# Attention steps in four places of a group, a reordered head, and the last down weights in w_ops

## The chip, the cores and the metric

The kernel runs on one core of a Trainium2 chip. Its time is the device time of one execution in microseconds; a profiled execution also gives a span, from the first to the last instruction, and a record of each engine: TensorE (PE), VectorE (DVE), ScalarE (ACT), GpSimd (POOL) and SyncE (SP), which here issues all DMAs.

## What is computed

```python
x = L0_attn_x                        # 1 x 2048 x 512, float32
xn = _layernorm(x, axis=-1)
# attention "over the heads of one token": 32 query heads, 8 key and value heads, D = 16
q = einsum('bse,edh->bsdh', xn, Wq) + bq
k = einsum('bse,edh->bsdh', xn, Wk) + bk   # k and v repeated 4 times along h
v = einsum('bse,edh->bsdh', xn, Wv) + bv
scores = einsum('bsdh,bseh->bsde', q, k) / sqrt(D)
s = einsum('bsde,bseh->bsdh', softmax(scores), v).reshape(...)
# gated feed-forward, inner size 1792
nx = xn * rsqrt(mean(xn * xn) + 1e-5) * ln_w
y = (silu(nx @ gate_w.T) * (nx @ up_w.T)) @ down_w.T
out = x + s * silu(y)
```

Scores are 16 x 16 for each token, so attention is no work for TensorE: VectorE does it by products and reductions.

## The kernel before

Each float32 operand is split into a high part (rounded to a format of TensorE, written by ACT) and a low part (the rest, written by VectorE or GpSimd); a product is then three matmuls, high x high, high x low, low x high. The 2048 rows go in 2 pairs of 1024; a pair is two blocks of 512 (4 tiles of 128 each). The inner size is 14 chunks of 128, so there are `GROUPS` = 28 groups: a group is one chunk of one pair, for both blocks.

**A group.** Gate and up for both blocks are a 2 x 2 block product, done in seven products in the manner of Strassen (m1 to m7, 6 matmuls of 512 columns each) instead of eight; groups 0 and 14 are plain (gate0, up0, gate1, up1, 12 matmuls each). TensorE's order in a group is m1, m5, m6, m2, m7, one down product (12 matmuls), m4, m3: 54 matmuls. Between them ACT copies the running sum into another bank (`seed`, L782, for which m6 waits), `take_u2` (L797, for m7), `silu0`, `take_u3`, and `silu1` of the group before (L806). VectorE does `c12` of the group before behind its m3 (L1068), `times_up1` of the group before (L1079), `c22` (L1064) and `times_up0` (L1073, which needs m4). ACT's `h_hi_part` and GpSimd's `h_lo_part` (L413) then split the product h.

**Weights.** In the first pair each chunk's weights are loaded raw, scaled, combined (`sums`, L1028) and split (`hi_a`, `lo_a`, `hi_s`, `lo_s`; `hi_wd` and GpSimd's `wd_lo_part` for the down weights), and written to DRAM; later use loads them back. `w_ops` has two slots of chunk weights, `wd_ops` three slots of down weights, filled in turn by `load_wd` (L309). There are `ITEMS` = 56 down products; those beyond 41 come behind the last group.

**Attention.** A tile's attention is 13 steps of VectorE, in one fixed sequence over all tiles (`attn_place`): six for scores (product, reduction, product, reduction, row maximum, subtraction) and seven for values (product, reduction, product, reduction, row sum, reciprocal, scaling). Between them ACT takes an exponential for a pair of tiles (`exps`, L827), for which the first value step waits; exponential and silu need different tables on ACT. There are 208 steps. `attention(n)` (L1131) runs the next n. `PAIR_SHARES` (L240) says how many run at each of three places of each group, `BURST_SHARES` at nine places between the pairs; what is left runs behind the last group.

**Head.** Before group 1 the first eight tiles of x are normalised and transposed, QKV is computed for them (`qkv_product`, taken from the bank by VectorE's `qkv_take`), and four combined operands are made: `t_add` (DVE), `t_hi` (ACT), `t_lo` (DVE). The order on every engine is written out by hand; waits are counts of semaphores. Each engine runs its instructions in that order, so a waiting one holds up all behind it.

**End.** `y_out` (ACT, L833) takes the silu of an output tile; `finish` (DVE, L1139) multiplies it by the attention result and adds x; SyncE stores it.

## Time and profile before

| | us |
|---|---|
| median of 3 runs | 500.21 (499.72 to 500.76) |
| profiled execution | 499.32 |
| its span | 497.5 |
| TensorE busy | 474.6 (95%) |
| VectorE busy | 409.6 (82%) |
| ScalarE busy | 229.3 (46%) |
| GpSimd busy | 121.7 (24%) |

The mean granted clock of TensorE is 0.991 of full speed. Busy time counts each engine by itself; the engines overlap. Matmuls are pipelined: one is shown longer than the distance to the next, and the distance is its cost. Where an engine stood idle before a row, the row may end with the idle time and with what ended it.

### The profile page before, as it was taken

Reading aid. Unit: us, or ns where it says so; the run is one execution under the profiler, and the core shown is the slowest. Engines: PE = TensorE matmul, PEld = TensorE weight load, DVE = VectorE, ACT = ScalarE, POOL = GpSimd, SP = SyncE. Lnnn points to the kernel's source line nnn. Section 1 sums busy time; section 2 is a strip of 40 time slices with the busy share of each in tenths; the row PEclk is TensorE's granted clock in tenths of the full one; section 3 lists DMA queues with packets and bytes.
Section 4 is the critical chain, followed back from the end, with each engine's and each line's share of the span. In section 5 each row is a group of like instructions: output and inputs, shape, how many; then the busy total and the mean of one; then the engine's idle time right before and its main releaser. Section 6 shows DMA issues by size and latency. Waiting matters only on the chain.

```text
span 497.5 us, 6152 instructions
## 1 busy us (share of the span) xinstructions
PE 474.6 (95%) x2148; PEld 392.4 (79%) x2148; DVE 409.6 (82%) x538; ACT 229.3 (46%) x379; POOL 121.7 (24%) x104
## 2 busy tenths in 40 slices
PE   7797999999999999999999999999999999999980
PEld 6696888778778888888898888888888888888870
DVE  7679688888898798749999767986888697699996
ACT  4683565576577554394114263224322532547010
POOL 3713121121222182242232111111111111139600
PEclk9999999999999999999999999999999999999996
DMA  8802799666666755683354559555556545415552
GB/s 280 301 1 88 283 319 393 239 250 251 238 248 241 273 221 209 230 343 114 121 186 164 190 193 359 192 199 219 207 198 214 224 182 198 163 50 203 182 200 85
DMA packets 27311, 105.12 MB, mean 211 GB/s; under 512 B 2833, under 2 KB 4113, under 8 KB 23953
## 3 DMA queue, kind: packets, MB, share of 16 engines
q1 hardware_dynamic: 27280, 104.74, 57.6%
q8 instruction: 17, 0.28, 0.2%
q14 instruction: 14, 0.11, 0.1%
HBM read 68.29 MB, written 36.44 MB: 210 GB/s over the span
## 4 chain that ended last, share of the span: by engine, by line
PE 68%; DVE 15%; issue 8%; ACT 3%; SPq 2%; POOL 2%; DMA 1%; DVEq 0%; ACTq 0%; POOLq 0%
PE gu_ps L469 14%; PE gu_ps L472 13%; PE gu_ps L471 13%; PE y_ps L596 6%; PE y_ps L598 6%; PE y_ps L597 6%; DVE prod L1119 2%; PE gu_ps L618 2%; PE gu_ps L619 2%; PE gu_ps L622 2%; DVE attn L1122 2%; DVE prod L1101 2%; DVE xz L1146 1%; DMA bias<-bv 1%; SPq L266 1%
## 5 line engine op out<-in xcount | busy, mean ns | idle before, releaser
L469 PE MATMUL gu_ps<-z_hi,w_ops 128*128 128x512 f32 x364 | 143.3, 394 | 0.4
L472 PE MATMUL gu_ps<-z_hi,w_ops 128*128 128x512 f32 x364 | 141.8, 389 | 0.0
L471 PE MATMUL gu_ps<-z_lo,w_ops 128*128 128x512 f32 x364 | 141.7, 389 | 0.0
L420 POOL TENSOR_TENSOR h_lo<-h,h_hi 128x512 fp32r<-128x512 f32 x28 | 37.8, 1351 | 200.6 <-ACT h_hi L825 200.6
L469 PEld LDWEIGHTS gu_ps<-z_hi,w_ops 128*128 128x128 f32 x364 | 68.3, 188 | 19.7 <-ACT u L800 5.0
L472 PEld LDWEIGHTS gu_ps<-z_hi,w_ops 128*128 128x128 f32 x364 | 68.3, 188 | 14.3
L471 PEld LDWEIGHTS gu_ps<-z_lo,w_ops 128*128 128x128 f32 x364 | 68.3, 188 | 13.6
L596 PE MATMUL y_ps<-wd_ops,h_hi 128*128 128x512 f32 x168 | 65.9, 392 | 0.1
L598 PE MATMUL y_ps<-wd_ops,h_lo 128*128 128x512 f32 x168 | 65.6, 391 | 0.0
L597 PE MATMUL y_ps<-wd_ops,h_hi 128*128 128x512 f32 x168 | 65.5, 390 | 0.0
L825 ACT ACTIVATE h_hi<-h 128x512 fp32r<-128x512 f32 x28 | 17.7, 631 | 81.9 <-DVE h L1077 81.9
L1119 DVE TENSOR_TENSOR prod<-scores,qkv 128x1024 f32<-128x1024 f32 x32 | 43.5, 1358 | 0.8
L1101 DVE TENSOR_TENSOR prod<-qkv 128x1024 f32<-128x1024 f32 x32 | 42.9, 1341 | 0.5
L424 POOL TENSOR_TENSOR wd_ops<-raw,wd_ops 128x512 fp32r<-128x512 f32 x14 | 20.1, 1436 | 88.5 <-ACT wd_ops L748 88.5
L1122 DVE TENSOR_REDUCE attn<-prod 128x64 f32<-128x1024 f32 x32 | 38.9, 1216 | 0.8
L1104 DVE TENSOR_REDUCE scores<-prod 128x128 f32<-128x1024 f32 x32 | 38.9, 1216 | 0.8
L598 PEld LDWEIGHTS y_ps<-wd_ops,h_lo 128*128 128x128 f32 x168 | 31.5, 188 | 6.7
L596 PEld LDWEIGHTS y_ps<-wd_ops,h_hi 128*128 128x128 f32 x168 | 31.5, 188 | 6.6 <-POOL h_lo L420 0.3
L597 PEld LDWEIGHTS y_ps<-wd_ops,h_hi 128*128 128x128 f32 x168 | 31.6, 188 | 6.3
L1089 DVE TENSOR_TENSOR h_kept<-u 128x512 f32<-128x512 f32 x26 | 19.0, 730 | 19.4 <-ACT u L813 19.3
L420 POOL TENSOR_TENSOR h_lo<-h_kept,h_hi 128x512 fp32r<-128x512 f32 x15 | 20.3, 1354 | 45.1 <-ACT h_hi L825 45.1
L800 ACT ACTIVATE u<-gu_ps 128x512 f32<-128x512 f32 x26 | 15.6, 600 | 29.3 <-PE gu_ps L472 19.3
(120 smaller groups left out, 769.2 us busy)
## 6 DMA issues: line engine op xcount, KB each, us to landing
w_kept<-w_ops SPq DMA_DIRECT2D x13, 1792.0 KB, 5.7
w_ops<-w_kept SPq DMA_DIRECT2D x13, 1792.0 KB, 7.5
wd_ops<-wd_kept SPq DMA_DIRECT2D x42, 512.0 KB, 3.5
raw<-gate_up SPq DMA_DIRECT2D x28, 256.0 KB, 3.6
wd_kept<-wd_ops SPq DMA_DIRECT2D x14, 512.0 KB, 7.2
xz<-x SPq DMA_DIRECT2D x16, 256.0 KB, 5.9
raw<-down SPq DMA_DIRECT2D x14, 256.0 KB, 7.4
xz<-x SPq DMA_DIRECT2D x2, 1024.0 KB, 5.7
```

The lines of the kernel that those rows point to most:

```text
L420: pool.tensor_tensor(lo, src, hi.bitcast(F32), ALU.subtract).then_inc(h_lo_done, 1)
L424: pool.tensor_tensor(wd_ops[:, n % 3, 1, :], wd_raw[:, n % 2, :], wd_ops[:, n % 3, 0, :].bitcast(F32), ALU.subtract).then_inc(wd_lo_done, 1)
L469: pe.matmul(acc, w_h, z_hi[:, zi, c, :], start=start and c == 0, stop=False, skip_group_check=True)
L471: pe.matmul(acc, w_h, z_lo[:, zi, c, :], start=False, stop=False, skip_group_check=True)
L472: end = pe.matmul(acc, w_l, z_hi[:, zi, c, :], start=False, stop=c == 1, skip_group_check=True)
L596: pe.matmul(acc, hi, wd_ops[:, u % 3, 0, :], start=n == 0, stop=False)
L597: pe.matmul(acc, hi, wd_ops[:, u % 3, 1, :], start=False, stop=False)
L598: pe.matmul(acc, lo, wd_ops[:, u % 3, 0, :], start=False, stop=n == NI - 1).then_inc(d_done, 1)
L1101: return dve.tensor_tensor(pr, q[:, d:d + HALF, :].unsqueeze(2).to_broadcast([P, HALF, D, HKV]), k.unsqueeze(1).to_broadcast([P, HALF, D, ...
L1104: return dve.tensor_reduce(s[:, d:d + HALF, :], pr, X, ALU.add)
L1119: return dve.tensor_tensor(pr, e[:, d:d + HALF, :].unsqueeze(2).to_broadcast([P, HALF, HKV, D]), v.unsqueeze(1).to_broadcast([P, HALF, HKV ...
L1122: return dve.tensor_reduce(o[:, d:d + HALF, :], pr, X, ALU.add)
```

## The change

1. **Four places.** Each group has a fourth place for attention steps, behind `times_up0`. The table is new; it sums to 49 and 130 steps for the two pairs instead of 42 and 104, so with the burst's 29 all 208 are placed. For example group 15 has (0, 7, 3, 1) instead of (0, 3, 2), group 16 (0, 5, 3, 0) instead of (1, 5, 2), group 26 (0, 6, 4, 0) and group 27 (2, 6, 3, 1) instead of (1, 5, 2). In the first pair GpSimd's `wd_lo_part` also waits for the first reduction of its group's second place.
2. **Order in a group.** ACT does `silu1` ahead of `seed`; in the first pair `hi_wd` and mostly `hi_s` move forward, and VectorE does `times_up1` ahead of `sums`.
3. **Head.** The query weights come in two loads and are summed and split in halves; the biases are loaded ahead of x tiles 5 to 7; up0(0) starts on the high weights; QKV products 0 and 7, down product 0, and many operations of ACT and VectorE change places.
4. **Late down weights.** Down products 49 to 55 have seven places of their own in `w_ops`, loaded once m3 of the last group is done.

```diff
+        LATE = ITEMS - 7
+        w_late = w_ops[:].rearrange("p a s m n -> p (a s m n)").rearrange("p (u s n) -> p u s n", u=7, s=2)
+
+        def wd_place(u):
+            return w_late[:, u - LATE] if u >= LATE else wd_ops[:, u % 3]
...
+        PAIR_SHARES = (((0, 0, 0, 0), (0, 0, 0, 0), (0, 0, 1, 0), (1, 3, 2, 0), (1, 2, 1, 1), (0, 3, 1, 0),
...
+                       ((0, 3, 4, 0), (0, 7, 3, 1), (0, 5, 3, 0), (0, 6, 2, 0), (1, 6, 2, 1), (0, 5, 3, 0),
...
+        def first_reduce(g):
+            before = attn_before(g) + shares[g][0]
+            return next((q for q in range(before, before + shares[g][1]) if places[q][2] in (1, 3)), 0)
...
+            def load_late_wd(u):
+                sp.wait_ge(m3_done, GROUPS)
+                sp.dma_start(wd_place(u).rearrange("p s n -> p (s n)").bitcast(F32), wd_kept[item(u)[1]])\
+                  .then_inc(wd_late_loaded[u - LATE], 16)
...
-            sp.dma_start(wq_raw, wq.rearrange("(k p) n -> p k n", p=P)).then_inc(wq_in, 16)
+            for a in (0, 2):
+                sp.dma_start(wq_raw[:, a:a + 2, :], wq.rearrange("(k p) n -> p k n", p=P)[:, a:a + 2, :])\
+                  .then_inc(wq_in[a // 2], 16)
...
-            load_x(0, range(J, JJ))
+            load_x(0, (J,))
...
+            load_x(0, range(J + 1, JJ))
...
-            for u in range(ITEMS - NI, ITEMS):
+            for u in range(ITEMS - NI, LATE):
                 load_wd(u)
+            for u in range(LATE, ITEMS):
+                load_late_wd(u)
...
             def wd_lo_part(n):
                 pool.wait_ge(wd_hi_done, n + 1)
+                wait(pool, attn_step, first_reduce(n))
...
+            def first_up0():
+                pe.wait_ge(w_hi_a, 2)
+                for n, (wi, zi, c) in enumerate(chunks):
+                    w_h = w_ops[:, 0, 0, wi, c * P:(c + 1) * P]
+                    pe.matmul(acc, w_h, z_hi[:, zi, c, :], start=n == 0, stop=False)
+                    pe.matmul(acc, w_h, z_lo[:, zi, c, :], start=False, stop=False)
+                pe.wait_ge(w_lo_a, 2)
...
             first_gate0()
-            up0(0)
+            first_up0()
+            qkv_product(0)
             second_tile(J)
-            qkv_product(0)
+            qkv_product(1)
             second_tile(J + 1)
-            qkv_product(1)
             second_tile(J + 2)
...
-            for index in range(4, JJ - 1):
+            for index in range(4, JJ):
                 qkv_product(index)
-            down_product(0)
...
+            h_hi_part(0)
+            hi_wd(0)
             z_hi_tile(0, J + 3)
...
+            t_hi(0, 0)
             silu1(0)
-            h_hi_part(0)
-            for n in range(3):
-                t_hi(0, n)
-            hi_wd(0)
+            t_hi(0, 1)
+            t_hi(0, 2)
             hi_s(1)
+            scale(2, (0, 1))
             t_hi(0, 3)
-            scale(2, (0, 1))
             for g in range(1, NI):
-                seed(g)
                 if g >= 2:
                     silu1(g - 1)
+                seed(g)
...
             for g in range(NI + 1, GROUPS):
-                seed(g)
                 if g > NI + 1:
                     silu1(g - 1)
+                seed(g)
...
                 attention(shares[g][2])
                 times_up0(g)
+                attention(shares[g][3])
             c12(LAST)
             times_up1(LAST)
-            attention(6)
-            assert taken[0] >= values_end(3 * J - 1)
+            attention(STEPS)
             for j in range(J):
                 finish(2, j)
-                attention(4)
-            attention(STEPS)
```

How the instructions stand in a row, at three places. First ACT at the start of group 4, before and after; the row with `h_hi<-h` ends group 3's work, `gu_ps<-gu_ps` is the seed, `u<-u` is `silu1` (its wait: `c12_done`), `w_ops<-raw` of 768 is `hi_a`:

```order
L825 ACTIVATE h_hi<-h 128x512 [waits d_done,h0_done]
L788 ACTIVATE gu_ps<-gu_ps 128x512 [waits c12_done,m1_done]
L813 ACTIVATE u<-u 128x512 [waits c12_done]
L735 ACTIVATE w_ops<-raw 128x768 [waits gu_scaled,w_stored1,m3_done]
L800 ACTIVATE u<-gu_ps 128x512 [waits h1_done,m6_done]
L795 ACTIVATE h<-gu_ps 128x512 [waits h_lo_done,m2_done]
L804 ACTIVATE u<-gu_ps 128x512 [waits m7_done]
```

```order
L868 ACTIVATE h_hi<-h 128x512 [waits d_done,h0_done]
L856 ACTIVATE u<-u 128x512 [waits c12_done]
L831 ACTIVATE gu_ps<-gu_ps 128x512 [waits c12_done,m1_done]
L778 ACTIVATE w_ops<-raw 128x768 [waits gu_scaled,w_stored1,m3_done]
L791 ACTIVATE wd_ops<-raw 128x512 [waits wd_stored1,d_done,wd_in0]
L843 ACTIVATE u<-gu_ps 128x512 [waits h1_done,m6_done]
L838 ACTIVATE h<-gu_ps 128x512 [waits h_lo_done,m2_done]
```

`silu1` and the seed have changed places, and `hi_wd` has come forward.

Then VectorE near the end of the head, before (from `t_lo` to the takes of QKV products 5 and 6) and after (from the last of the sums to the last operation ahead of group 1); `z_lo<-h_kept` is `t_lo`, `h_kept<-h_kept` is `t_add`, `qkv<-gu_ps` a take, `h_kept<-u,gu_ps` is `times_up1(0)`:

```order
L1025 TENSOR_TENSOR z_lo<-h_kept,z_hi 128x1024 [waits t_hi_done]
L1020 TENSOR_TENSOR h_kept<-h_kept 128x2x512 [waits t_added]
L1025 TENSOR_TENSOR z_lo<-h_kept,z_hi 128x1024 [waits t_hi_done] x2
L1042 TENSOR_TENSOR w_ops<-raw,w_ops 128x768 [waits w_hi_a]
L1061 SCALAR_TENSOR_TENSOR qkv<-gu_ps,rms,bias 128x384 [waits rms_done,qkv_done]
L1033 TENSOR_TENSOR raw<-raw 128x256 [waits gu_scaled]
L1034 TENSOR_TENSOR raw<-raw 128x256
L1036 TENSOR_TENSOR raw<-raw 128x256 [waits w_summed]
L1038 TENSOR_TENSOR raw<-raw 128x256 [waits w_summed]
L1089 TENSOR_TENSOR h_kept<-u,gu_ps 128x512 [waits m3_done,silu1_done]
L1061 SCALAR_TENSOR_TENSOR qkv<-gu_ps,rms,bias 128x384 [waits rms_done,qkv_done] x2
```

```order
L1089 TENSOR_TENSOR raw<-raw 128x256 [waits w_summed]
L1140 TENSOR_TENSOR h_kept<-u,gu_ps 128x512 [waits m3_done,silu1_done]
L1112 SCALAR_TENSOR_TENSOR qkv<-gu_ps,rms,bias 128x384 [waits rms_done,qkv_done]
L1076 TENSOR_TENSOR z_lo<-h_kept,z_hi 128x1024 [waits t_hi_done]
L1112 SCALAR_TENSOR_TENSOR qkv<-gu_ps,rms,bias 128x384 [waits rms_done,qkv_done]
L1076 TENSOR_TENSOR z_lo<-h_kept,z_hi 128x1024 [waits t_hi_done]
L1100 TENSOR_TENSOR w_ops<-raw,w_ops 128x1024 [waits w_hi_s]
L1112 SCALAR_TENSOR_TENSOR qkv<-gu_ps,rms,bias 128x384 [waits rms_done,qkv_done]
L1076 TENSOR_TENSOR z_lo<-h_kept,z_hi 128x1024 [waits t_hi_done]
L1112 SCALAR_TENSOR_TENSOR qkv<-gu_ps,rms,bias 128x384 [waits rms_done,qkv_done]
L1071 TENSOR_TENSOR h_kept<-h_kept 128x2x512 [waits t_added]
```

The take of product 4 now stands ahead of all `t_lo`, and the fourth `t_add` is the last operation of the head.

Then VectorE in group 15, from `t_lo(1, 3)` (`z_lo<-raw`) to its c12 before, and from the same operation to the last step ahead of `times_up0(15)` after; `u<-gu_ps,u` is c22 (wait `u3_done`) or c12:

```order
L1025 TENSOR_TENSOR z_lo<-raw,z_hi 128x1024 [waits t_hi_done]
L1119 TENSOR_TENSOR prod<-scores,qkv 128x1024 [waits attn_step]
L1122 TENSOR_REDUCE attn<-prod 128x64 [waits attn_step]
L1124 TENSOR_REDUCE row_sum<-scores 128x16 [waits attn_step]
L1066 TENSOR_TENSOR u<-gu_ps,u 128x512 [waits u3_done]
L1126 RECIPROCAL row_inv<-row_sum 128x16 [waits attn_step]
L1127 TENSOR_TENSOR attn<-attn,row_inv 128x128 [waits attn_step]
L1077 TENSOR_TENSOR h<-h,gu_ps 128x512 [waits silu0_done,m4_done]
L1071 TENSOR_TENSOR u<-gu_ps,u 128x512 [waits u2_done,m3_done]
```

```order
L1076 TENSOR_TENSOR z_lo<-raw,z_hi 128x1024 [waits t_hi_done]
L1170 TENSOR_TENSOR prod<-scores,qkv 128x1024 [waits attn_step]
L1173 TENSOR_REDUCE attn<-prod 128x64 [waits attn_step]
L1175 TENSOR_REDUCE row_sum<-scores 128x16 [waits attn_step]
L1177 RECIPROCAL row_inv<-row_sum 128x16 [waits attn_step]
L1178 TENSOR_TENSOR attn<-attn,row_inv 128x128 [waits attn_step]
L1152 TENSOR_TENSOR prod<-qkv 128x1024 [waits qkv_out,attn_step]
L1155 TENSOR_REDUCE scores<-prod 128x128 [waits attn_step]
L1117 TENSOR_TENSOR u<-gu_ps,u 128x512 [waits u3_done]
L1152 TENSOR_TENSOR prod<-qkv 128x1024 [waits attn_step]
L1155 TENSOR_REDUCE scores<-prod 128x128 [waits attn_step]
L1157 TENSOR_REDUCE row_max<-scores 128x16 [waits attn_step]
```

Ten steps stand between `t_lo(1, 3)` and `times_up0(15)`, where five stood.

## Rows read from the trace of the kernel before

**Rows 1.** The page, busy us, share of the span and instructions of each engine.

```profile
PE 474.6 (95%) x2148; PEld 392.4 (79%) x2148; DVE 409.6 (82%) x538; ACT 229.3 (46%) x379; POOL 121.7 (24%) x104
```

**Rows 2.** Who waited for whom (us in total, times, longest).

```profile
PE gu_ps L618 <- issue: 3.5, 1, 3.5
PE gu_ps L488 <- DVE w_ops L1042: 2.5, 1, 2.5
```

**Rows 3.** Timeline of the end: start us, duration us, engine, line, operation, tiles.

```profile
480.42 0.47 PE L596 MATMUL gu_ps<-wd_ops,z_hi 128*128 128x512 f32 x1 [1.26 <-DMA wd_ops<-wd_kept]
...
485.00 1.23 DVE L1119 TENSOR_TENSOR prod<-scores,qkv 128x1024 f32<-128x1024 f32 x1
...
485.75 0.39 PE L598 MATMUL gu_ps<-wd_ops,z_lo 128*128 128x512 f32 x1
486.17 0.60 ACT L841 ACTIVATE xz<-gu_ps 128x512 f32<-128x512 f32 x1 [0.76 <-PE gu_ps L598]
486.26 1.22 DVE L1122 TENSOR_REDUCE attn<-prod 128x64 f32<-128x1024 f32 x1
...
488.47 0.68 DVE L1146 TENSOR_TENSOR xz<-xz,attn 128x512 f32<-128x512 f32 x1
...
493.24 0.69 DVE L1150 TENSOR_TENSOR xz<-xz 128x512 f32<-128x512 f32 x1
```

**Rows 4.** Timeline between the pairs and of group 14.

```profile
269.04 0.63 ACT L831 ACTIVATE scores<-scores 128x512 f32<-128x512 f32 x1
...
277.30 0.68 DVE L1077 TENSOR_TENSOR h<-h,gu_ps 128x512 f32<-128x512 f32 x1
...
280.44 0.39 PE L488 MATMUL gu_ps<-z_hi,w_ops 128*128 128x512 f32 x1
...
283.15 0.39 PE L469 MATMUL gu_ps<-z_hi,w_ops 128*128 128x512 f32 x1
...
286.29 1.23 DVE L1025 TENSOR_TENSOR z_lo<-raw,z_hi 128x1024 fp32r<-128x1024 f32 x1 [2.15 <-ACT z_hi L780]
```

**Rows 5.** The page, DMA issues: count, KB each, median us from issue to landing.

```profile
wd_ops<-wd_kept SPq DMA_DIRECT2D x42, 512.0 KB, 3.5
```

**Rows 6.** Timeline of the head, all engines.

```profile
13.90 0.63 ACT L735 ACTIVATE w_ops<-raw 128x512 fp32r<-128x512 f32 x1
...
15.62 0.67 DVE L1042 TENSOR_TENSOR w_ops<-raw,w_ops 128x512 fp32r<-128x512 f32 x1
...
16.35 0.50 PE L488 MATMUL gu_ps<-z_hi,w_ops 128*128 128x512 f32 x1 [2.46 <-DVE w_ops L1042]
...
30.29 3.62 DVE L1020 TENSOR_TENSOR h_kept<-h_kept 128x1024 f32<-128x1024 f32 x3 [0.67 <-ACT h_kept L770]
...
42.85 0.60 DVE L1061 SCALAR_TENSOR_TENSOR qkv<-gu_ps,rms,bias 128x384 f32<-128x384 f32 x1
...
43.55 0.41 PE L618 MATMUL gu_ps<-wqkv_hi,z_hi 128*128 128x384 f32 x1 [3.53 <-issue]
```

**Rows 7.** Timeline of group 4, where m7 starts late.

```profile
86.83 1.34 POOL L420 TENSOR_TENSOR h_lo<-h,h_hi 128x512 fp32r<-128x512 f32 x1 [4.81 <-ACT h_hi L825]
86.93 1.52 DVE L1034 TENSOR_TENSOR raw<-raw 128x256 f32<-128x256 f32 x1
...
89.94 0.60 ACT L800 ACTIVATE u<-gu_ps 128x512 f32<-128x512 f32 x1 [1.31 <-DVE h_kept L1089]
...
90.60 0.50 PE L469 MATMUL gu_ps<-z_hi,w_ops 128*128 128x512 f32 x1
```

**Rows 8.** Groups 15 to 26: stretch and length, busy us of PE, PEld, DVE, ACT, POOL.

```profile
283.15:431.13 147.98, 147.98 (x649) 121.31 (x648) 115.27 (x145) 56.42 (x87) 14.25 (x11) 1.00 0.59 217
```

**Rows 9.** Timeline of ACT and VectorE at the end of group 26.

```profile
429.98 0.69 DVE L1077 TENSOR_TENSOR h<-h,gu_ps 128x512 f32<-128x512 f32 x1 [1.24 <-PE gu_ps L472]
...
431.33 0.69 DVE L1071 TENSOR_TENSOR u<-gu_ps,u 128x512 f32<-128x512 f32 x1 [0.67 <-PE gu_ps L472]
...
433.29 1.28 ACT L813 ACT_TABLE_LOAD   x1
```

More of the change, by code:

```diff
@@ L443, in _ @@
                 .then_inc(bias_summed, 1)
-            scale_tile(J + 1)
-            pool.wait_ge(var_done, J + 1)
-            rms_of(0, J, 1, 0)
-            scale_tile(J + 2)
-            scale_tile(J + 3)
+            for j in range(J + 1, JJ):
+                scale_tile(j)
             pool.wait_ge(var_done, JJ + 2)
@@ L514, in first_gate0 @@
                 end.then_inc(m2_done, 1)
+            def first_up0():
+                acc = gu_ps[:, UP_BANK, :]
+                chunks = [(wi, zi, c) for wi, zi in ((WA21, ZB11), (WA22, ZB21)) for c in range(2)]
+                pe.wait_ge(w_hi_a, 2)
[4 more added lines that the diff above has]
+                pe.wait_ge(w_lo_a, 2)
+                for n, (wi, zi, c) in enumerate(chunks):
+                    end = pe.matmul(acc, w_ops[:, 0, 1, wi, c * P:(c + 1) * P], z_hi[:, zi, c, :], start=False,
+                                    stop=n == 3)
+                end.then_inc(m4_done, 1)
             def up0(g):
-                if g:
-                    pe.wait_ge(c12_done, sevens(g))
-                else:
-                    pe.wait_ge(w_lo_a, a_pieces(0))
+                pe.wait_ge(c12_done, sevens(g))
                 eight(gu_ps[:, UP_BANK, :], g, ((WA21, ZB11), (WA22, ZB21))).then_inc(m4_done, 1)
@@ L845, in _, with hi_qkv @@
             act.wait_ge(lnw_in, 16)
+            def hi_qkv(half_of_k):
+                k = slice(2 * half_of_k, 2 * half_of_k + 2)
+                act.wait_ge(wqkv_summed, 2 * half_of_k + 2)
+                act.wait_ge(wkv_in, 32)
+                act.activation(wqkv_hi[:, k, :], wqkv_raw[:, k, :], ACT.Copy).then_inc(wqkv_hi_done, 1)
             scale(0, (0,))
@@ L860, in _ @@
             silu0(0)
+            z_tile(J)
             z_tile(J + 1)
@@ L1208, in _ @@
                 attention(shares[g][0])
-                if g + 1 < NI:
-                    sums(g + 1)
                 if g > 1:
@@ L1213, in _ @@
                 if g + 1 < NI:
+                    sums(g + 1)
                     lo_a(g + 1, WA11, WS1, a_pieces(g + 1))
+                if g == 1:
+                    t_lo(0, 3)
                 if g == 8:
@@ L1228, in _ @@
                 c22(g)
-                if g == 1:
-                    qkv_take(JJ - 1)
                 if g + 1 < NI:
```

121 lines of the change are left out of this document (63 added, 58 removed), and 4 rows, old and new, of the table PAIR_SHARES.

## The prediction

> **What bounds the kernel now.** I read the page's engine line first: TensorE is busy 474.6 of 497.5 us [rows 1], so time can only come from its few gaps and from what lies behind its last matmul. The list of who TensorE waited for gives two large gaps, 3.5 us before a QKV product and 2.5 us before up0(0) [rows 2]; a third, 1.26 us for a down weight, stands in the timeline of the end [rows 3]. In that timeline the last matmul starts at 485.75, the last `y_out` on ACT at 486.17, but VectorE is still doing attention steps; its first closing product starts at 488.47 and its last addition at 493.24, ending at 493.93, and the span ends 3.57 us later with the last store [rows 3]. So the end is set by VectorE, not by TensorE. From 60 us on TensorE runs group after group of 54 matmuls. A matmul of 512 columns starts 0.227 us after the one before: 12 of them, up1(14), take 280.44 to 283.15 [rows 4]. A group is then 12.25 us. I write times inside a group from its first m1 matmul.
>
> **The tail, -5.7.** The new table sums to 179 steps and the burst adds 29: 208, all there are. Before, 33 steps were left behind the last group; a product or a reduction starts 1.26 us after the step ahead of it (485.00, 486.26) [rows 3]. With none left, the last two VectorE operations follow the last `y_out`: 486.17 + 0.60, then 0.7 + 0.7 with their hand-overs, 488.25. Before it was 493.93: -5.7. The four closing pairs take 1.35 us each and the four `y_out` come 1.36 us apart, so they keep pace. The store behind them is unchanged.
>
> **Late down weights, -1.4.** Products 49 to 55 get places of their own in `w_ops`. The wait at 480.42 (1.26 us idle, 1.4 against the pace) goes [rows 3], unless the seven loads come late. On SyncE they stand behind load 48, which waits for product 45; load 49 is then wanted three products (8.2 us) later, and each further one 2.7 us later. A load of this size takes 3.5 us to land (median of 42) [rows 5], so the queue has room. If that cover failed, the old 1.3 us would be back.
>
> **The head, -3.0.** The old up0(0) waited for both halves of its weights. Its high half is ready when ACT ends at 14.53, the low half when VectorE ends at 16.29, and TensorE starts at 16.35 [rows 6]. `first_up0` asks for the high half alone: start 14.6, -1.75. A part is lost again: by my estimate the low QKV weights, now in two pieces with statistics between them, are ready only near 19.2, and gate1(0) waits for the last `z_lo` near 29.2, which follows its `z_hi` on ACT behind `h_hi(0)` and `hi_wd(0)`. I get up1(0) done 1.0 earlier. The 3.5 us gap at 43.55 is a wait for `qkv_take(4)`, which VectorE does at 42.85, behind additions, `t_lo` and `lo_a` [rows 6]. In the new order I start `t_add` at 29.85 instead of 30.29 and add up by like rows: the first addition 1.2 and 0.8 of blocking by `h_lo(0)`, a take 0.55, two additions 2.4 (three took 3.62 [rows 6]), `lo_a` 0.9 (0.67 for two thirds of it at 15.62), four sums 1.45 (0.42 each, overlapping), `times_up1` 0.6, take 0.55, so 38.3. TensorE wants it at 38.8: the gap (3.7 with its restart) goes. But ACT has `t_hi(0, 3)` ahead of `seed(1)`, and `t_add(0, 3)` is now the last operation of VectorE's head, ending near 45.7. The chain behind take 4 is three `t_lo` of 1.2, three takes, `lo_s` 1.1 and that addition, 7.4. With 1.06 for `t_hi` and 0.58 for the seed, m6(1) can start at 47.35, and TensorE is there at 45.65: +1.7. In sum -1.0 - 3.7 + 1.7 = -3.0. Bounds: -4.7 if the seed isn't late, -1.3 if VectorE's head slips 1.7 more (one contended operation costs about 1.1: 1.52 at 86.93 where the same takes 0.42 [rows 7]). The split query load and the earlier RMS cost nothing: behind them ACT waits for the value weights anyway.
>
> **Groups 2 to 13, -2.2.** m7 waits for `u2`, `u2` for `times_up1`, and that stood behind four sums: in group 4 ACT ends `u2` at 90.54 and m7 starts at 90.60, 0.25 behind pace, with 0.1 more at the restart [rows 7]. Five groups have that in full and two in part, with small ones 1.9 in all. `silu1` and `times_up1` now come first, 1.5 us earlier. VectorE's work in the fullest groups (3 and 7) is 5.9 for weights and products and 5.9 attention, 11.8 of 12.25, and `h_lo` on GpSimd runs beside a reduction there. So I take these waits as gone. Group 13's late `times_up0` goes with them (-0.3).
>
> **Groups 15 to 27: -1.1 and +3.8.** The same m7 wait (0.22 in five groups) goes. What comes is VectorE's load. In groups 15 to 26 it was busy 115.3 of 148.0 us [rows 8]; steps added there cost 20.8 more, 136.1 of 147.0. Bounded from the rows of an ordinary group, `times_up0` can start at 11.1, c12 at 12.45 (0.20 of the next) [rows 9]. Where they come late:
> - Burst. It now ends with two value steps of pair 2, which wait for an exponential that ACT reaches only at 269.04 to 269.67 [rows 4]; VectorE is there near 264.8 and stands 5 us. Then two steps, four closing pairs and three steps: `times_up0(14)` ends near 281.1, not 277.98. up1(14) wants it at 280.44: +0.7.
> - Group 15. `t_lo(1, 3)` can't start before 3.14 (286.29, group start 283.15) [rows 4]. Then 7 steps (5.97), c22, 3 steps (2.93): `times_up0` at 13.8 instead of 11.1, c12 at 14.8 instead of 12.45. silu1, seed and m6(16) follow 1.9 behind c12: +1.7.
> - Groups with an exponential (17, 20, 23, 26). ACT now loads the table (1.28, row 433.29 [rows 9]) ahead of the seed, so m6 can start 3.84 behind `times_up0`: just in time if that starts at 11.1, late by what it is late. 0.1 each in three, but group 26 has steps of 3.0 between c22 at 9.2 and `times_up0`: near 12.2, +1.1. Together +1.4.
>
> The sum on the profiled execution: -5.7 - 1.4 - 3.0 - 2.2 - 1.1 + 0.7 + 1.7 + 1.4 = -9.6, so a span of 487.9. The execution took 499.32 where the runs' median is 500.21; I set the forecast against the median: 490.6, rounded 490.5.
>
> **Contention.** A VectorE operation with two inputs in SBUF that meets one of GpSimd waits for it: `raw` at 86.93 took 1.52 instead of 0.42, ending just behind GpSimd's at 88.17 [rows 7]. The Trainium skill (SBUF — State Buffer, Who interferes with whom) states an exclusive lock: whoever is second blocks until the first is done, and reductions never meet it. By that rule the trace agrees; an estimate from it is one whole GpSimd operation for each meeting, against 1.1 from the row.
>
> **Rivals.**
> 1. *The places fit, nothing new is late* (seed in the head, groups 15 and 26 on time, burst too). For it: slack of 10.9 us in twelve groups. Against: the exponential and `t_hi` can't come earlier. It gives 490.5 - 1.7 - 3.8, 485.0. Chance 0.12.
> 2. *VectorE bounds part of the second half.* 136.1 and one meeting with `h_lo` in each of twelve groups (1.1 each) are 149.3 for 147.0: +2.3, and with the forced waits between places another 2. 494.5. Chance 0.10.
> 3. *The head gives next to nothing*: VectorE's head slips further and the first groups run late. +1.7 to +3: 493. Chance 0.10.
> 4. *Slower.* VectorE must wait in order: 0.66 us between `times_up0` and c12 and 0.78 (ACT's silu with its hand-overs) between c12 and `times_up1` where a place is empty [rows 9]. If each group pays 11.35 of work, 1.1 of blocking and both waits, it lasts 13.9 instead of 12.25: 12 x 1.65 is 19.7, less the 2.8 counted, near 507. It decides from 13.1 us a group. Against it: empty places are used in just those groups whose work is less, and blocking mostly meets a reduction. Chance 0.04.
> 5. *The late loads don't hide*, or come in another order: +1.4, 491.9. Inside my range; 0.04.
>
> **How the numbers follow.** The forecast keeps 0.60 (488 to 492.5). Rivals 1, 2 and 3 set the ends: 485.5 to 494.8 leaves out the slower case and a part of 1 and 2. A measurement of this kernel can tell 0.2% (1 us) from no change. Faster holds all but rival 4: 0.95; same 0.01; slower 0.04.
>
> **What would show it.** Right: VectorE's last operation within 1.6 us of the last `y_out`; no gap in the last 13 products; up0(0) near 14.6; no wait before QKV product 6 but one before m6(1) behind `t_hi` and `seed`; a VectorE idle of 5 us before a value product near 265; gaps before up1(14), m6(16), m6(27). Wrong: `times_up0` starting beyond 12 in most groups of the second half, or c12 beyond 13, or a span above 493.

## The result, and the profile after

| | before | changed |
|---|---|---|
| median, us | 499.97 (4 runs, 498.80 to 500.76) | 488.71 (4 runs, 488.14 to 488.76) |
| ratio of the times, 95% interval | | 0.977 (0.975 to 0.980) |
| profiled execution, its span | 499.32, 497.5 | 488.14, 486.4 |

The forecast was 490.5. The prediction's sum was made against the profiled execution: a span of 487.9 was foretold, and 486.4 was measured. Busy time on the page of the changed kernel, the line that answers to [rows 1]:

```profile
PE 473.5 (97%) x2148; PEld 394.6 (81%) x2148; DVE 395.4 (81%) x539; ACT 227.1 (47%) x378; POOL 119.4 (25%) x106
```

TensorE has the same work in 11 us less. What it waited for, in all 486 us (us in total, times, longest), against [rows 2]; two waits of 0.3 and 0.2 us are left out:

```profile
PE gu_ps L502 <- ACT gu_ps L831: 3.6, 4, 1.2
PE y_ps L687 <- POOL ident L419: 1.5, 1, 1.5
PE gu_ps L539 <- ACT z_hi L806: 1.2, 1, 1.2
PE gu_ps L521 <- DVE z_lo L1051: 0.9, 1, 0.9
PE gu_ps L521 <- DVE h L1128: 0.5, 1, 0.5
```

The waits of 3.5 and 2.5 us are gone. What is left is mostly one kind: m6 (L502) waits four times for the seed (L831).

Where the 11.1 us of span went is read from the start of the same down product in both timelines. In the changed kernel down product 1 (in group 2), 12 (in group 13), 27 (between the halves of group 14) and the first one behind the last group start at

```profile
63.12 0.39 PE L643 MATMUL y_ps<-wd_ops,h_hi 128*128 128x512 f32 x1
...
198.04 0.39 PE L643 MATMUL y_ps<-wd_ops,h_hi 128*128 128x512 f32 x1
...
268.61 0.39 PE L643 MATMUL y_ps<-wd_ops,h_hi 128*128 128x512 f32 x1
...
440.87 0.39 PE L643 MATMUL gu_ps<-wd_ops,h_hi 128*128 128x512 f32 x1
```

where the kernel before has 67.08, 204.37, 275.00 and 443.62. The lead is 3.96, 6.33, 6.39 and 2.75, and 4.31 at the last matmul (481.44, before 485.75). The entries are rounded one by one, and so don't add up to the last digit:

| stretch | prediction | measured |
|---|---|---|
| head, up to group 2 | -3.0 | -4.0 |
| groups 2 to 13 | -2.2 | -2.4 |
| groups 14 to 27 | +2.7 | +3.6 |
| last down weights | -1.4 | -1.6 |
| VectorE behind the last matmul | -5.7 | -5.7 |
| from VectorE's end to the span's end | 0 | -1.1 |
| sum | -9.6 | -11.1 |

The first row holds the start of the execution too: the first gate product begins at 11.45 in this trace and at 10.92 in the one before, so counted from there the head gave 4.5.

The end of the changed kernel, which answers to [rows 3]:

```profile
481.44 0.39 PE L645 MATMUL gu_ps<-w_ops,z_lo 128*128 128x512 f32 x1
481.87 0.60 ACT L884 ACTIVATE xz<-gu_ps 128x512 f32<-128x512 f32 x1 [0.76 <-PE gu_ps L645]
...
483.23 0.69 DVE L1201 TENSOR_TENSOR xz<-xz 128x512 f32<-128x512 f32 x1
```

VectorE's last operation starts 1.8 us behind the last matmul, before it was 7.5. The last `y_out` now sets it.

### The profile page after: what moved, and what is told of

It is laid out like the page before. It is cut to its first block, busy times and chain, and to the rows that moved or that the text cites. A ratio compares the mean times of both kernels' runs of the same rounds, so it can differ in the third digit from the quotient of the medians.

```text
span 486.4 us, 6166 instructions
## 1 busy us (share of the span) xinstructions
PE 473.5 (97%) x2148; PEld 394.6 (81%) x2148; DVE 395.4 (81%) x539; ACT 227.1 (47%) x378; POOL 119.4 (25%) x106
## 4 chain that ended last, share of the span: by engine, by line
PE 77%; DVE 11%; ACT 5%; issue 4%; DMA 1%; SPq 0%; POOL 0%; ACTq 0%; DVEq 0%
PE gu_ps L502 15%; PE gu_ps L505 15%; PE gu_ps L504 15%; PE y_ps L643 7%; PE y_ps L645 7%; PE y_ps L644 7%; PE gu_ps L644 3%; PE gu_ps L643 3%; PE gu_ps L645 3%; DVE prod L1170 1%; PE gu_ps L665 1%; PE gu_ps L666 1%; PE gu_ps L669 1%; DVE attn L1173 1%; DVE z_lo L1076 1%
## 5 line engine op out<-in xcount | busy, mean ns | idle before, releaser
L502 PE MATMUL gu_ps<-z_hi,w_ops 128*128 128x512 f32 x364 | 142.4, 391 | 3.6 <-ACT gu_ps L831 3.6
L447 POOL TENSOR_TENSOR h_lo<-h,h_hi 128x512 fp32r<-128x512 f32 x28 | 38.9, 1389 | 226.3 <-ACT h_hi L868 226.3
L502 PEld LDWEIGHTS gu_ps<-z_hi,w_ops 128*128 128x128 f32 x364 | 68.3, 188 | 20.8 <-issue 6.5
L1170 DVE TENSOR_TENSOR prod<-scores,qkv 128x1024 f32<-128x1024 f32 x32 | 41.8, 1308 | 5.5 <-ACT scores L874 4.8
L1152 DVE TENSOR_TENSOR prod<-qkv 128x1024 f32<-128x1024 f32 x32 | 40.5, 1265 | 0.6
L453 POOL TENSOR_TENSOR wd_ops<-raw,wd_ops 128x512 fp32r<-128x512 f32 x14 | 18.6, 1328 | 64.8 <-ACT wd_ops L791 28.7
L1197 DVE TENSOR_TENSOR xz<-xz,attn 128x512 f32<-128x512 f32 x16 | 15.4, 962 | 21.5 <-ACT xz L884 21.5
L1140 DVE TENSOR_TENSOR h_kept<-u 128x512 f32<-128x512 f32 x26 | 20.0, 771 | 14.2 <-ACT u L856 10.7
```

Of the source, the lines that this page charges most:

```text
L447: pool.tensor_tensor(lo, src, hi.bitcast(F32), ALU.subtract).then_inc(h_lo_done, 1)
L502: pe.matmul(acc, w_h, z_hi[:, zi, c, :], start=start and c == 0, stop=False, skip_group_check=True)
L1140: dve.tensor_tensor(h_kept[:, g % NI, :], u2[:], up, ALU.mult).then_inc(h1_done, 1)
L1152: return dve.tensor_tensor(pr, q[:, d:d + HALF, :].unsqueeze(2).to_broadcast([P, HALF, D, HKV]), k.unsqueeze(1).to_broadcast([P, HALF, D, ...
L1170: return dve.tensor_tensor(pr, e[:, d:d + HALF, :].unsqueeze(2).to_broadcast([P, HALF, HKV, D]), v.unsqueeze(1).to_broadcast([P, HALF, HKV ...
```

## The experiments

All are timed in five rounds beside the kernel before. "Against changed" is the difference to the changed kernel's 488.7, which was measured in other rounds: the kernel before had a median of 499.97 beside it, and of 499.9 to 501.1 beside the others. The last column says which of the texts written before the run came true, the theory or its rival.

| kernel | edit | us | ratio to before (95%) | against changed | result |
|---|---|---|---|---|---|
| up0_waits | changed, up0(0) late | 488.7 | 0.976 (0.974 to 0.978) | 0.0 | theory |
| seed_first | changed, seed(1) first | 487.7 | 0.974 (0.972 to 0.977) | -1.0 | theory |
| table_ahead | changed, silu table early | 486.4 | 0.971 (0.969 to 0.973) | -2.3 | theory |
| places_old | changed, old table and end | 491.7 | 0.982 (0.980 to 0.984) | +3.0 | theory, size off |
| late_off | changed, old slots | 490.2 | 0.981 (0.979 to 0.982) | +1.5 | theory |
| fit15 | changed, burst eased | 487.1 | 0.975 (0.973 to 0.976) | -1.6 | half |
| order_old2 | changed, seed before silu1 | 489.4 | 0.979 (0.977 to 0.981) | +0.7 | first's sign, half its size |
| zhi_first | changed, z_hi first | 488.3 | 0.977 (0.975 to 0.979) | -0.4 | rival, nearly |
| wdlo_free | changed, wd_lo unbound | 490.7 | 0.982 (0.980 to 0.984) | +2.0 | between |
| before_places | before, new places | 497.6 | 0.995 (0.993 to 0.996) | | theory's total, not its terms |
| before_late | before, late weights | 499.9 | 0.999 (0.997 to 1.000) | | theory |
| all_eased | changed, five edits | 482.4 | 0.964 (0.962 to 0.966) | -6.3 | theory |

The start of a profiled execution (when the first gate product begins) varied over these traces from 10.7 to 12.6 us, before any edit acts. The changed kernel's own interval is 0.975 to 0.980. Those of table_ahead, places_old and all_eased lie clear of it and that of wdlo_free touches it; the others overlap it. So for differences under 2 us the starts and gaps of TensorE in the traces decide, and the times only agree with them.

### The head

```diff
             def first_up0():
+                pe.wait_ge(w_lo_a, 2)
...
+            stats_tile(J)
             lo_a(0, WA22, WA21 + 1, 2)
             for j in range(J, JJ):
-                stats_tile(j)
+                if j > J:
+                    stats_tile(j)
```

> The changed kernel (488.7 us, span 486.4) with one part of the head undone: VectorE does the statistics of x tile 4 ahead of the low up weights again, and up0(0) waits for both halves of its weights. My theory: what up0(0) gains by starting early is not what the head gained. The changed kernel's TensorE waits 1.10 us before gate1(0), for a z_lo that does not hang on up0(0), and 0.46 before the first QKV product's low weights. So up0(0) will start near 16.3 instead of 14.3, gate1(0) at 28.8 to 29.3 instead of 28.83, and m6(1) at 46.7 as now, since its seed stands behind t_hi(0,3), which waits for VectorE's fourth t_add. Time 488.7, +0.5 at most. Rival: the early start is carried through, then the time is 2.0 longer, 490.7.

TensorE's first up product and m6(1) in this run:

```profile
15.45 0.50 PE L556 MATMUL gu_ps<-z_hi,w_ops 128*128 128x512 f32 x1 [1.13 <-DVE w_ops L1094]
...
46.55 0.47 PE L502 MATMUL gu_ps<-z_hi,w_ops 128*128 128x512 f32 x1 [1.04 <-ACT gu_ps L832]
```

up0(0) starts 1.2 later than the changed kernel's 14.29 (not 2.0: x tile 4 was there earlier than before), and m6(1) not later than its 46.70. The early start of up0(0) is worth nothing by itself: the next wait, 1.10 us before gate1(0) in the changed kernel, takes it up (0.21 here).

```diff
+            seed(1)
             t_hi(0, 3)
             for g in range(1, NI):
                 if g >= 2:
                     silu1(g - 1)
-                seed(g)
+                    seed(g)
```

> The changed kernel with seed(1) ahead of t_hi(0,3) on ScalarE, nothing else. My theory: m6(1) waits 1.2 us in the changed kernel only because the seed stands behind t_hi(0,3), which ends at 45.97, while m1(1) is done near 44.1. With the seed first the gap before m6(1) goes, and m4(1), which needs the t_lo of that t_hi, has 6 us more: -1.2, so 487.5 and a span of 485.2. Rival: t_lo(0,3) or the takes behind it are what is late next, in m4(1) or group 2, and less than 0.3 is gained: 488.6.

The changed kernel first: VectorE's fourth `t_add`, ScalarE's `t_hi` and seed, and m6(1).

```profile
43.76 1.22 DVE L1071 TENSOR_TENSOR h_kept<-h_kept 128x1024 f32<-128x1024 f32 x1
...
45.01 1.06 ACT L823 ACTIVATE z_hi<-h_kept 128x1024 fp32r<-128x1024 f32 x1 [5.83 <-DVE h_kept L1071]
45.98 0.58 ACT L831 ACTIVATE gu_ps<-gu_ps 128x512 f32<-128x512 f32 x1
...
46.70 0.47 PE L502 MATMUL gu_ps<-z_hi,w_ops 128*128 128x512 f32 x1 [1.05 <-ACT gu_ps L831]
```

And the seed of the other kernel:

```profile
45.45 0.58 ACT L831 ACTIVATE gu_ps<-gu_ps 128x512 f32<-128x512 f32 x1 [5.12 <-PE gu_ps L505]
```

The seed now waits for TensorE (m1), not TensorE for the seed: of four long m6 waits three are left. In the changed kernel a wait of ScalarE for VectorE, 5.8 us long, had stood ahead of the seed, which needs nothing of it.

```diff
+            z_hi_tile(0, J + 3)
             h_hi_part(0)
             hi_wd(0)
-            z_hi_tile(0, J + 3)
```

> The changed kernel with z_hi of x tile 7 ahead of h_hi(0) and hi_wd(0) on ScalarE in the head. My theory: gate1(0) waits 1.10 us for the last z_lo, because its z_hi stands behind those two operations (26.42 to 27.56). With the z_hi first, that z_lo, the z_raw, the t_add behind it and the whole chain to t_hi(0,3) and m6(1) come 1.0 earlier: -1.0, so 487.7, with m6(1) at 45.7 instead of 46.70. Rival: h_hi(0) and hi_wd(0) then delay GpSimd's two operations into VectorE's t_add, or the chain hangs on other things, and the gap moves to QKV product 6 or stays before m6(1): no change, 488.7.

The gap before gate1(0) went, and the one before m6(1) grew by 0.3. GpSimd's `wd_lo(0)` and `h_lo(0)`, and two of VectorE's `t_add`, in order of time:

```profile
28.49 1.30 POOL L453 TENSOR_TENSOR wd_ops<-raw,wd_ops 128x512 fp32r<-128x512 f32 x1 [4.11 <-ACT wd_ops L791]
...
28.93 1.94 DVE L1071 TENSOR_TENSOR h_kept<-h_kept 128x1024 f32<-128x1024 f32 x1 [0.83 <-ACT h_kept L813]
...
29.74 2.29 POOL L447 TENSOR_TENSOR h_lo<-h,h_hi 128x512 fp32r<-128x512 f32 x1
...
31.32 1.79 DVE L1071 TENSOR_TENSOR h_kept<-h_kept 128x1024 f32<-128x1024 f32 x1
```

An addition takes 1.22 alone. Moved 0.5 earlier, VectorE met GpSimd twice (+0.7 and +0.6), where in the changed kernel it meets it once (+0.6), and lost again most of what it had won. The rival holds but for 0.3: the head hangs on VectorE's chain, not on gate1(0).

The largest part of the head's gain, the 3.7 us ahead of QKV product 6, was not undone by any run. The trace of the kernel before shows two causes. One is the prediction's: the take stands behind other work. The other it left out: in that stretch VectorE met GpSimd twice, a `t_lo` at 38.67 took 2.32 instead of 1.22, and the `lo_a` below 2.01 instead of 0.95, in sum 2.2 us.

```profile
39.87 2.24 POOL L420 TENSOR_TENSOR h_lo<-h,h_hi 128x512 fp32r<-128x512 f32 x1
...
40.91 2.01 DVE L1042 TENSOR_TENSOR w_ops<-raw,w_ops 128x768 fp32r<-128x768 f32 x1
```

In the changed kernel ScalarE does `h_hi(0)` and `hi_wd(0)` early, GpSimd is done with both of its operations at 30.15, and from there on VectorE's chain up to that take meets nothing: its next additions take 2.47 for two, its `lo_a` 0.95. How the 3.7 us divide between the place of the take and these meetings no run shows.

### The places and the end

```diff
-        PAIR_SHARES = (((0, 0, 0, 0), (0, 0, 0, 0), (0, 0, 1, 0), (1, 3, 2, 0), (1, 2, 1, 1), (0, 3, 1, 0),
...
+        PAIR_SHARES = (((0, 0, 0, 0), (0, 1, 1, 0), (0, 2, 2, 0), (0, 2, 2, 0), (0, 2, 2, 0), (0, 2, 2, 0),
...
-            attention(STEPS)
+            attention(6)
             for j in range(J):
                 finish(2, j)
+                attention(4)
+            attention(STEPS)
```

> The changed kernel with the old table of attention steps (three places, 42 and 104 steps) and the old end with 33 steps left behind the last group; the new orders, head and late weights stay. My theory: the end gives back 5.7 us (7.5 instead of 1.8 between TensorE's last matmul and VectorE's last addition) and perhaps 1 of the last store, while the second pair, whose groups lost 3.7 against the kernel before in the changed kernel, runs at 12.25 a group without a gap: -4.8. So 488.7 + 6.8 - 4.8 = 490.7, and TensorE's last matmul starts near 476.7 instead of 481.4. Rival: the load that the steps put on the groups costs nothing (the gaps in groups 15 to 27 come from the new order on ScalarE alone): then 488.7 + 6.8 = 495.5, last matmul at 481.4.

The last matmul and VectorE's last addition:

```profile
478.58 0.39 PE L644 MATMUL gu_ps<-w_ops,z_lo 128*128 128x512 f32 x1
...
486.88 0.69 DVE L1200 TENSOR_TENSOR xz<-xz 128x512 f32<-128x512 f32 x1
```

The end is 8.3 us behind the last matmul instead of 1.8, so 6.5 comes back. TensorE has no gap over 0.31 us from 150 us on; from down product 12 to the first product behind the last group it takes 4.1 us less than the changed kernel. That is the price of the new places, which the prediction put at 0.7 + 1.7 + 1.4 = 3.8. My expectation for the total missed by 1.0. It put the price at 4.8, 0.7 too high, and this trace was 1.2 us later than the changed kernel's already at down product 12, of which 0.5 is the start of the execution. The other way went the last store: it let that come back 1 us later, which it didn't (2.4 us from VectorE's end to the span's end here too), while VectorE's end gave back 6.5 and not 5.7.

```diff
-        LATE = ITEMS - 7
+        LATE = ITEMS
```

> The changed kernel with the last seven down products loaded into the three slots of wd_ops again, nothing else. My theory: the wait for the last load (1.26 us idle, 1.4 with its restart, row at 480.42 of the kernel before) comes back at the down product before the last two, and nothing behind it has slack: +1.4, so 490.1. Rival: the seven late loads are slow themselves (7.8 us to land instead of 3.5, six at once beside the products) and cost TensorE something that the gaps don't show, so that the old slots lose less than 0.5: 489.2 at most.

```profile
478.77 0.47 PE L643 MATMUL gu_ps<-wd_ops,z_hi 128*128 128x512 f32 x1 [1.37 <-DMA wd_ops<-wd_kept]
```

One wait, of 1.37 idle and 1.5 against the pace, and the time is 1.5 longer. Then the same part alone on the kernel before:

> The kernel before with one part of the change alone: the last seven down products in places of their own. In the changed kernel that part is worth 1.5 us (490.2 without it, 488.7 with it). My theory: the worth hangs on what comes last. In the kernel before VectorE's attention steps end 7.5 us behind the last matmul, and nothing of them waits for TensorE, so the 1.4 us wait at the last products is hidden: TensorE's last matmul starts at 484.3 instead of 485.75 and the time stays, 500.0 within 0.3, as far as the start of the runs allows. Rival: the two add, as the prediction's sum has them, and the part gives -1.4 here too: 498.6.

The trace shows the wait gone, the last matmul 2.4 us earlier than in [rows 3] (1.5 of it from this wait, the rest from a head with smaller waits for x), but VectorE only 0.9 earlier:

```profile
483.30 0.39 PE L615 MATMUL gu_ps<-w_ops,z_lo 128*128 128x512 f32 x1
...
492.36 0.69 DVE L1167 TENSOR_TENSOR xz<-xz 128x512 f32<-128x512 f32 x1
```

The measured ratio of 0.999 reaches from -1.3 to 0 us, so the time alone would not exclude the rival by much; that TensorE's 1.5 us stay ahead of a VectorE that doesn't wait for it is in the trace. That part is worth its 1.5 us only once VectorE's steps have left the end.

The other part alone, the new table with the fourth place and the new end, on the kernel before (the table is left out below):

```diff
+                attention(shares[g][3])
...
-            attention(6)
-            assert taken[0] >= values_end(3 * J - 1)
+            attention(STEPS)
             for j in range(J):
                 finish(2, j)
-                attention(4)
-            attention(STEPS)
```

> The kernel before with one part of the change alone: the new table with the fourth place and the end without steps left behind. Old head, old orders, old slots for the last down weights. My theory: -5.7 at the end, and the load in the groups of the second pair costs what it cost with the old order on ScalarE: gaps of 3.6 us from group 15 on (measured in the changed kernel with the old order) and 0.8 before up1(14), against 1.6 that the kernel before has there: +2.8. Sum -2.9: 0.6% under the kernel before, 497.1 where that takes 500.0. Rival: without the other edits the new places hold up the first pair as well (groups 3 and 7 are full, and times_up1 stands behind the sums), 2 us more, 499.

0.55% under the kernel before (0.36 to 0.74), 2.7 us, near the 2.9 of the theory. But the terms are other ones. Here VectorE's last operation starts 1.8 us behind the last matmul (-5.7), and the wait for the last weights, 1.5 us, is now on the path. From down product 12 to the first one behind the last group TensorE takes 243.7 us instead of 239.3, +4.4, where the theory had +2.8. Against that stand 1.2 us won in groups 2 to 13 (136.1 instead of 137.3 from down product 1 to 12), by the new table alone, which nothing here foretold, and 0.5 won ahead of them. That the total came out is luck. By themselves the new places give back half of what they take from the end.

### The exponential groups

```diff
                 exps(exps_in(g))
+                if exps_in(g):
+                    act.activation(scratch[:, 1:2], scratch[:, 0:1], ACT.Silu).then_inc(table_loaded, 1)
```

> The changed kernel with a silu of one column behind each group's exponentials in groups 15 to 27, so that ScalarE loads the silu table while it waits for times_up0, and not between c12 and silu1. My theory: in the groups with an exponential (17, 20, 23, 26) the table load of 1.28 us stands ahead of silu1 and of the seed; the gaps before m6(18) (0.64) and m6(27) (1.00), and small ones before m6(21) and m6(24), go: -1.8, so 486.9, span 484.6. Rival: VectorE's late times_up0 and c12 cause these gaps by themselves, and the load only adds to what is late anyway: then half of it or less goes, -0.8, 487.9.

The changed kernel at the end of group 26, in order: `times_up0`, `h_hi`, the table load, `silu1`, the seed, m6(27).

```profile
427.33 0.68 DVE L1128 TENSOR_TENSOR h<-h,gu_ps 128x512 f32<-128x512 f32 x1
428.05 0.63 ACT L868 ACTIVATE h_hi<-h 128x512 fp32r<-128x512 f32 x1 [3.21 <-DVE h L1128]
428.69 1.28 ACT L856 ACT_TABLE_LOAD   x1
...
429.99 0.63 ACT L856 ACTIVATE u<-u 128x512 f32<-128x512 f32 x1
430.53 0.58 ACT L831 ACTIVATE gu_ps<-gu_ps 128x512 f32<-128x512 f32 x1
431.25 0.47 PE L502 MATMUL gu_ps<-z_hi,w_ops 128*128 128x512 f32 x1 [0.84 <-ACT gu_ps L831]
```

ScalarE waited 3.2 us for `times_up0`, and loaded the table after it. With the load moved into that idle time, the load and the seed:

```profile
424.39 1.28 ACT L993 ACT_TABLE_LOAD   x1
...
428.72 0.58 ACT L831 ACTIVATE gu_ps<-gu_ps 128x512 f32<-128x512 f32 x1
```

`times_up0` is no earlier in its group (426.87, with group 26's down product at 421.6 instead of 422.1), yet the seed is in time. No gap before m6(18), m6(21), m6(24) or m6(27) is left: 2.3 us. The load is the cause; VectorE's lateness alone does no harm there.

The Trainium skill (ScalarE: Activation LUTs, What ACT_TABLE_LOAD costs) states about 2.66 us for a switch, of which 1.38 is a drain. Here the switch costs 1.31: `h_hi` ends at 428.68 and `silu1` starts at 429.99, with nothing between them but the load.

```diff
-                if g > NI + 1:
-                    silu1(g - 1)
                 seed(g)
+                if g > NI + 1:
+                    silu1(g - 1)
```

> The changed kernel with the seed ahead of silu1 on ScalarE in groups 16 to 27, as before; the new places stay. What the prediction says: the m7 waits of 0.22 come back in about five groups, +1.1, so 489.8. What the run with the early table load has shown since: the gaps before m6(18), m6(21), m6(24) and m6(27) come from the table load ahead of the seed. In the old order the seed doesn't wait for it: these gaps (2.0 in sum) go and 0.6 of the one before m6(16), against the m7 waits of up to 1.1; then -1.5, 487.2. The sign tells which weighs more.

The sign is the first expectation's, and the size about half of it: +0.7 by the times, and +0.6 in the trace, where TensorE takes 156.8 us from the down product of group 15 to the first one behind the last group and the changed kernel 156.2. (The gaps of more than 0.13 us alone add up to 3.2 us from 290 us on in both and don't show it; what is lost at each restart has to be counted too.) From one down product to the next the old order wins 0.5 each up to those of groups 16, 18 and 27, and loses 0.2 to 0.9 up to those of groups 19, 22, 24 and 25. The load in the exponential groups changes its victim: it is no longer ahead of the seed but ahead of `silu1`, so VectorE waits longer for that before `times_up1`, and its c22 comes late for m3. VectorE's wait for `silu1` (total, times, longest), with the old order and in the changed kernel:

```profile
DVE h_kept L1140 <- ACT u L856: 22.1, 20, 2.5
```

```profile
DVE h_kept L1140 <- ACT u L856: 10.7, 14, 1.3
```

```profile
328.12 0.50 PE L502 MATMUL gu_ps<-z_hi,w_ops 128*128 128x512 f32 x1 [0.20 <-DVE u L1117]
```

That is the wait for c22 in the old order (0.36 against the pace), and there is another at 365.60. So `silu1` first is the better order here by 0.6 us. How the two orders compare with the table loaded ahead no run shows.

### The burst and group 15

```diff
-                       ((0, 3, 4, 0), (0, 7, 3, 1), (0, 5, 3, 0), (0, 6, 2, 0), (1, 6, 2, 1), (0, 5, 3, 0),
+                       ((0, 7, 3, 0), (0, 5, 2, 1), (0, 5, 3, 0), (0, 6, 2, 0), (1, 6, 2, 1), (0, 5, 3, 0),
...
-            exps(exps_in(NI))
+                if u == NI + 11:
+                    exps(exps_in(NI)[:1])
+                if u == NI + 12:
+                    exps(exps_in(NI)[1:])
```

> The changed kernel with two exponentials of the burst done earlier on ScalarE (the first behind h_hi 25, the second behind h_hi 26, instead of both behind h_hi 27), and three attention steps moved from group 15 to group 14: (0,7,3,0) and (0,5,2,1) instead of (0,3,4,0) and (0,7,3,1). My theory: VectorE stood 4.6 us for the first exponential and was then late for times_up0(14) and, with the full group 15, for times_up0(15). With both eased the gap before up1(14) (0.70, with its restart 0.8) and the one before m6(16) (1.35) go: -2.1, so 486.6, span 484.3. Rival: t_lo(1,3), which must wait for t_hi(1,3) behind up1(14), keeps group 15 late whatever stands behind it; then only -0.8 shows, 487.9.

The changed kernel: VectorE's value product behind its wait for the exponential, and up1(14).

```profile
263.39 1.23 DVE L1170 TENSOR_TENSOR prod<-scores,qkv 128x1024 f32<-128x1024 f32 x1 [4.62 <-ACT scores L874]
...
274.75 0.50 PE L521 MATMUL gu_ps<-z_hi,w_ops 128*128 128x512 f32 x1 [0.54 <-DVE h L1128]
```

With the edit:

```profile
259.31 2.27 DVE L1173 TENSOR_TENSOR prod<-scores,qkv 128x1024 f32<-128x1024 f32 x1
...
275.17 0.50 PE L521 MATMUL gu_ps<-z_hi,w_ops 128*128 128x512 f32 x1 [0.45 <-DVE h L1131]
```

The value product comes 4.1 earlier and the gap before m6(16) (1.35) is gone, with 0.4 of the one before m6(18). But up1(14) still waits 0.6: I had put seven steps ahead of `times_up0(14)` instead of three, 3.9 us in place of the time won, and the first met GpSimd (2.27 for 1.23). With five steps there, in the last kernel below, the wait is gone: the number of steps was wrong here, not the mechanism.

### GpSimd beside VectorE

```diff
-                wait(pool, attn_step, first_reduce(n))
```

> The changed kernel without GpSimd's wait for the first reduction ahead of wd_lo in groups 1 to 13. wd_lo then starts when ScalarE's hi_wd is done, near 3 us into the group, beside VectorE's operations with two inputs. My theory, from the rows of the kernel before (an operation of 0.42 that took 1.52 beside GpSimd's): each of 12 groups pays about 1 us more of VectorE, 10 to 12 us of busy time, but groups with slack hide it, and only the full ones (3 and 7) and those with a late c22 pass it on: +0.5, so 489.2. Rival: it is on the path in each group, through lo_a and c22, and TensorE waits in most: +3 or more, 492. Other rival: the meetings cost nothing here, VectorE's busy time stays within 1 us, 488.7.

GpSimd's `wd_lo` at the start of group 5 and VectorE's `lo_a` beside it; then that `lo_a` in the changed kernel, where `wd_lo` waits until 98.95 and lies beside a reduction:

```profile
96.78 1.41 POOL L452 TENSOR_TENSOR wd_ops<-raw,wd_ops 128x512 fp32r<-128x512 f32 x1 [1.92 <-ACT wd_ops L790]
...
96.96 2.04 DVE L1092 TENSOR_TENSOR w_ops<-raw,w_ops 128x768 fp32r<-128x768 f32 x1
```

```profile
96.72 0.95 DVE L1093 TENSOR_TENSOR w_ops<-raw,w_ops 128x768 fp32r<-128x768 f32 x1
```

1.1 us for one meeting, as in [rows 7]. VectorE's busy time grew by 8.5 us, and most groups hid their share, but three did not: 1.09 before m6(6), 0.65 and 0.18 later, in sum the 2.0 measured. The first is in the group behind one with an exponential again, where the table load (106.79) stands ahead of the seed:

```profile
109.34 0.47 PE L501 MATMUL gu_ps<-z_hi,w_ops 128*128 128x512 f32 x1 [0.93 <-ACT gu_ps L830]
```

My "full groups 3 and 7" were the wrong ones: in the group of the largest gap what decides is not VectorE's sum but how late `times_up0` may be, and an exponential takes 1.3 us off that; the second gap, before m3(9), is a late c22. One wait on GpSimd, which the prediction costed at nothing, holds 2.0 us of the gain.

### Together

The edits of seed_first, table_ahead and zhi_first, the exponentials of fit15, and

```diff
-                       ((0, 3, 4, 0), (0, 7, 3, 1), (0, 5, 3, 0), (0, 6, 2, 0), (1, 6, 2, 1), (0, 5, 3, 0),
+                       ((0, 5, 5, 0), (0, 5, 2, 1), (0, 5, 3, 0), (0, 6, 2, 0), (1, 6, 2, 1), (0, 5, 3, 0),
```

> The changed kernel with the eased places together: seed(1) ahead of t_hi(0,3), the silu table loaded behind the exponentials, z_hi of tile 7 first, the two exponentials of the burst earlier, and shares (0,5,5,0) and (0,5,2,1) in groups 14 and 15, so that five steps and not seven stand ahead of times_up0(14). My theory: each removes a wait of its own. Against the changed kernel: seed -1.0 and table -2.3 as measured alone; up1(14) -0.8 and m6(16) -1.35, of which the run before had the second; z_hi -0.3. Sum -5.7, so 483.0, span 481.1, and no gap of TensorE over 0.2 us from 250 us on. Rival: the waits share VectorE's lateness, and easing one shows the next; then less than 4 is gained, 485 or more.

```profile
PE y_ps L687 <- POOL ident L419: 1.5, 1, 1.5
PE gu_ps L669 <- DVE wqkv_lo L1212: 0.9, 1, 0.9
PE gu_ps L539 <- ACT z_hi L806: 0.8, 1, 0.8
PE y_ps L678 <- DVE xz L1027: 0.6, 2, 0.3
PE y_ps L643 <- POOL h_lo L447: 0.2, 1, 0.2
```

That is TensorE's whole list of waits in a span of 479.8 us: 482.4 us, 6.3 under the changed kernel and 3.6% under the one before. No wait is left in the groups, and no gap over 0.2 us from 20 us on except two of 0.31 and 0.22. The gains added up (5.7 foretold), so they were separate waits. VectorE's share is not the bound: it is busy 396.9 us here and 395.4 in the changed kernel.

## Why the prediction was right

- **What bounds the kernel.** Right: the end was VectorE's and is TensorE's now.
- **The tail, -5.7.** -5.7, and VectorE's last operation starts 1.36 us behind the last `y_out`, inside the 1.6 foretold.
- **Late down weights, -1.4.** -1.6 in the table, -1.5 undone. The sum was right as a whole, but its two terms aren't separate: without the first the second is hidden (before_late).
- **The head, -3.0.** Mechanism right in the main, 1.0 too small. No wait before QKV product 6, up0(0) at 14.29 (14.6 foretold), and the wait before m6(1) stands behind `t_hi` and the seed. VectorE's chain ran shorter than the sum of like rows: `t_add(0, 3)` ended at 44.98, not 45.7, so that wait is 1.2 and not 1.7; gate1(0) began 1.36 earlier than before, not 1.0. But up0(0) had no part in it (up0_waits), and the account of the 3.5 us gap left out VectorE's two meetings with GpSimd, 2.2 us in all.
- **Groups 2 to 13, -2.2.** -2.4, but the terms are off. The trace of the kernel before has four groups with the m7 wait in full and two in part, not five and two, and each costs 0.5 and 0.25 to 0.3 from down product to down product: 2.6 over the pace in all and not 1.9, of which 0.3 is left. Nor is the new order the only way to it: with the old table the changed kernel is 2.1 under the kernel before there (places_old), and with the old orders the new table alone gives 1.2 (before_places). And 2.0 of it rest on a wait that I had not costed (wdlo_free).
- **m7 in groups 15 to 27, -1.1.** Too large. The new order gave 0.5 with the old table (places_old: 238.8 us from down product 12 to the first one behind the last group, the kernel before 239.3) and 0.6 with the new one (order_old2).
- **Group 15, +1.7, and the burst, +0.7.** 1.35 and 0.7, at the places foretold; with restarts 0.2 more. VectorE stood 4.6 us for the exponential, where 5 was foretold.
- **The step that failed: exponential groups, +1.4.** They cost 2.3 (table_ahead), the largest error inside the groups. I took m6 to be just in time if `times_up0` starts 11.1 into the group and gave three of four groups 0.1. But the step ahead of it is a product of 1.2 us, and in group 17, which starts at 303.84, `times_up0` starts 11.7 in: m6(18) comes 3.9 behind it, as foretold (3.84), and so waits 0.64 and not 0.1. Group 26 was right (1.0, foretold 1.1).

```profile
315.53 0.68 DVE L1128 TENSOR_TENSOR h<-h,gu_ps 128x512 f32<-128x512 f32 x1
...
319.45 0.47 PE L502 MATMUL gu_ps<-z_hi,w_ops 128*128 128x512 f32 x1 [0.49 <-ACT gu_ps L831]
```

- **The last store.** -1.1 that no term had, below.
- **Luck.** The head's surplus of 1.0 and the 0.9 that groups 14 to 27 cost over the sum nearly cancel. What is left of the miss on the span, 1.5 us, is mostly the store.
- **Rivals.** VectorE does not bound the second half: with its full load all gaps there go (all_eased). The one that came nearest is the first, that nothing new is late; its 485.0 is passed once five edits are made (482.4), not before.
